# A transformer block in hand-written engine orders: the first and last rounds written out anew

## What is computed

```python
ada = silu(c) @ W_ada + b_ada
shift_msa, scale_msa, gate_msa, shift_mlp, scale_mlp, gate_mlp = jnp.split(ada, 6, axis=-1)
h = _modulate(_layernorm(x), shift_msa, scale_msa)
x = x + gate_msa * _attention(h, W_qkv, b_qkv, W_proj, b_proj)
h = _modulate(_layernorm(x), shift_mlp, scale_mlp)
mlp = jax.nn.gelu(h @ W_fc1 + b_fc1, approximate=True) @ W_fc2 + b_fc2
x = x + gate_mlp * mlp
```

## Time and profile before

| | us |
|---|---|
| median of 3 runs | 1245.8 (1245.76 to 1247.27) |
| the profiled execution's own time | 1245.94 |
| its span | 1244.2 |
| TensorE busy | 1189.1 (96%) |
| VectorE busy | 902.8 (73%) |
| ScalarE busy | 866.3 (70%) |
| GpSimd busy | 541.5 (44%) |

### The profile page before, as it was taken

One profiled execution on the slowest core, in us unless ns is written; L12 is line 12 of the kernel. 1 busy time (PEld: TensorE's weight loads), 2 busy tenths in 40 slices (PEclk: granted clock), 3 DMA queues, 4 the chain that ended last, 5 costly groups with the idle time before them and its releaser, 6 DMA issues.

```text
span 1244.2 us, 27564 instructions
## 1 busy us (share of the span) xinstructions
PE 1189.1 (96%) x9863; PEld 1074.2 (86%) x9863; DVE 902.8 (73%) x1928; ACT 866.3 (70%) x1485; POOL 541.5 (44%) x557
## 2 busy tenths in 40 slices
PE   5877899999999999999999999999999999999987
PEld 5655799999999999999999999999999999998777
DVE  5367777777787777777877777778777877776642
ACT  3186777777777777777777777777777777777721
POOL 3001344455444444544444455444444444444454
PEclk9689999999999999999999999999999999999999
DMA  9344454555554555554454555545455555454220
GB/s 261 111 129 142 145 169 153 165 163 162 164 167 136 161 159 166 165 164 159 154 157 157 160 165 161 167 157 162 147 157 164 162 165 164 149 160 143 96 67 20
DMA packets 134330, 188.91 MB, mean 152 GB/s; under 512 B 24544, under 2 KB 102422, under 8 KB 133947
## 3 DMA queue, kind: packets, MB, share of 16 engines
q1 hardware_dynamic: 134195, 187.15, 47.6%
HBM read 121.92 MB, written 64.63 MB: 150 GB/s over the span
## 4 chain that ended last, share of the span: by engine, by line
PE 88%; DMA 3%; SPq 3%; ACT 2%; DVE 1%; issue 1%; POOL 1%; POOLq 0%; ACTq 0%; DVEq 0%
PE x_bank L585 11%; PE a_bank L677 10%; PE score_bank L615 10%; PE st_bank L632 9%; PE turn_bank L644 9%; PE b_bank L677 8%; PE b_bank L691 6%; PE b_bank L692 6%; PE b_bank L693 6%; PE a_bank L658 5%; PE x_bank L598 4%; SPq L432 1%; PE x_bank L563 1%; PE a_bank L563 1%; DMA o_rows<-on 1%
## 5 line engine op out<-in xcount | busy, mean ns | idle before, releaser
L943 DVE TENSOR_REDUCE mx<-score_bank 128x2 f32<-128x512 f32 x512 | 342.5, 686 | 110.0 <-PE score_bank L615 107.5
L762 ACT ACTIVATE e<-st_bank 128x1024 f32<-128x1024 f32 x256 | 262.6, 1026 | 136.0 <-PE st_bank L632 134.3
L1095 POOL TENSOR_TENSOR gl<-gl_raw,gh 128x512 fp32r<-128x512 f32 (+1 forms) x160 | 193.9, 1220 | 223.2 <-DVE gh L1013 223.2
L755 ACT CAST ql<-mxt 4x256 fp32r<-4x256 f32 x512 | 206.2, 403 | 11.6 <-DVE mxt L957 4.9
L615 PEld LDWEIGHTS score_bank<-kl,ql 122*128 122x128 f32 x1024 | 148.1, 192 | 43.7 <-issue 23.9
L615 PE MATMUL score_bank<-kl,ql 122*128 122x256 f32 x1024 | 175.4, 294 | 8.5 <-DMA ql<-zeros 6.2
L691 PE MATMUL b_bank<-w,gh 128*128 128x288 f32 x576 | 175.0, 304 | 2.9 <-POOL gl L1095 1.5
L632 PE MATMUL st_bank<-ql,kl 122*128 122x512 f32 x512 | 166.8, 407 | 11.0 <-ACT e L762 6.3
L692 PE MATMUL b_bank<-w,gh 128*128 128x288 f32 x576 | 171.1, 297 | 0.0
L693 PE MATMUL b_bank<-w,gl 128*128 128x288 f32 x576 | 170.9, 297 | 0.0
L644 PE MATMUL turn_bank<-e,ve 128*32 128x256 f32 x2048 | 123.8, 382 | 2.1 <-ACT e L762 2.1
(11 more groups left out here) (144 smaller groups left out, 2490.3 us busy)
## 6 DMA issues: line engine op xcount, KB each, us to landing
qk_rows<-qst SPq DMA_DIRECT2D x128, 256.0 KB, 5.4
ql<-qk_rows SPq DMA_DIRECT2D x384, 72.0 KB
kl<-qk_rows SPq DMA_DIRECT2D x384, 72.0 KB
o_rows<-on SPq DMA_DIRECT2D x128, 128.0 KB
gate<-gates SPq DMA_DIRECT2D x32, 432.0 KB, 4.7
xin<-in_x SPq DMA_DIRECT2D x32, 288.0 KB, 5.7
x<-in_x SPq DMA_DIRECT2D x32, 288.0 KB, 2.9
out<-x SPq DMA_DIRECT2D x32, 288.0 KB, 4.4
```

The lines of the kernel that those rows point to most:

```text
L755: last = nc.scalar.copy(rows[:, :, :, t, a, :], src)
L762: nc.scalar.activation(e[:, j % 4, :, :, :].rearrange("p u i l -> p (u i l)"), st_bank[:, :, :, :].rearrange("p u i l -> p (u i l)"), ACT. ...
L943: nc.vector.tensor_reduce(mx[:, j // HP, i, :, col:col + 1], score_bank[i][:, :].rearrange("p (t l) -> p t l", t=NT), AX.X, ALU.max).then_ ...
L1095: nc.gpsimd.tensor_tensor(gl[:, cols], g[:, cols], gh[:, cols].bitcast(F32), ALU.subtract).then_inc(g_lo, 1)
```

## The change

Each engine gets two more lists, a head with explicit batches for everything that rounds -2 to 2 did, and a tail with batches counted from the end for everything from round 30 on. `run` walks the head, then the old list for k = 3 to 29, then the tail. The steps in head and tail are the same as before but for these:

- The late prologue pieces become steps: `mod` and `gate2`, `gate5` on TensorE, `round` on ScalarE, `split`, `gates` and `mod` on VectorE.
- qk part 1 of batch 0 goes to b_bank. Part n of batch 0 waits for n // 2 drained parts.
- qk of every batch waits for the high part of its operand; only the fifth matmul waits for the low part, and the seventh for the remainder.
- Six of the first half's 12 row reads of batch 0 (its k rows) are started by ScalarE, as steps `qkr`.

```diff
-def run(order, steps):
+def run(head, order, tail, steps):
 
-    first = -max(off for _name, off, _n in order)
-    last = B - min(off for _name, off, _n in order)
-    for k in range(first, last):
+    for name, b, n in head:
+        steps[name](b, n)
+    last = B - (TAIL_PERIODS if tail else min(off for _name, off, _n in order))
+    for k in range(HEAD_PERIODS, last):
         for name, off, n in order:
             if 0 <= k + off < B:
                 steps[name](k + off, n)
+    for name, b, n in tail:
+        steps[name](B + b, n)
...
+        FIRST_LO = 4
+
+        def qk_bank(b, n):
+
+            return b_bank if b == 0 and n == 1 else x_bank
...
+        def qk_row(b, n):
+
+            half, m = n // READS, n % READS
+            slot, _use = half_use(b, half)
+            w, i, r = m // 6, m // 3 % 2, m % 3
+            part = ((0, 0, 1), (0, 1, 0))[w][r]
+            c0 = half * HALF_ROWS + (w * 2 + i) * D * HP
+            row = (0, HB)[i] + D * r
+            to = ql[row:row + D, slot, i, :, :] if w == 0 else kl[row:row + D, slot, :, :]
+            return (to.rearrange("p j l -> p (j l)").bitcast(F32),
+                    qk_dram[b % 2, part, c0:c0 + D * HP, :].rearrange("(d j) l -> d (j l)", j=HP))
...
+                if b == 0 and 6 <= n < 12:
+                    return
+                to, src = qk_row(b, n)
+                sp.dma_start(to, src).then_inc(qk_rows[slot], 16)
...
+            def second_mod(_b, _n):
+                pe.wait_ge(ada_rest, 16 * 3)
+                mod_columns(1)
+
             def gate_rows(v, k):
-
+                if k == 0:
+                    pe.wait_ge(ada_rest, 16 * 3)
+                    if v == 5:
+                        pe.wait_ge(x_drained, USE_QK + 2)
...
-                pe.wait_ge(x1_lo, b + 1)
-                pe.wait_ge(x1_rem, b + 1)
-                pe.wait_ge(x_drained, X_USES * b + USE_QK + n)
-                tiles, _rows, _ps = qk_tiles(n)
+                pe.wait_ge(x1_hi, 2 * b + 1)
+                pe.wait_ge(x_drained, X_USES * b + USE_QK + (n if b else n // 2))
+                tiles, _rows, _ps = qk_tiles(b, n)
+                bank = qk_bank(b, n)
                 for k, c in enumerate(tiles):
                     pr = products(xh1, xl1, xr1, wq)
                     for i, (xa, wa) in enumerate(pr):
-                        last = nc.tensor.matmul(x_bank[:, k * L:(k + 1) * L], wa[:, c * P:(c + 1) * P], xa,
+                        if n == 0 and k == 0 and i == FIRST_LO:
+                            pe.wait_ge(x1_lo, b + 1)
+                        if n == 0 and k == 0 and i == len(pr) - 1:
+                            pe.wait_ge(x1_rem, b + 1)
+                        last = nc.tensor.matmul(bank[:, k * L:(k + 1) * L], wa[:, c * P:(c + 1) * P], xa,
                                                 start=(i == 0), stop=(i == len(pr) - 1))
...
+            def first_k_rows(b, n):
+                if n == 0:
+                    for c in range(3):
+                        act.wait_ge(qk_stored[c], 16)
+                    act.wait_ge(consts, ROWS_SET)
+                to, src = qk_row(b, n + 6)
+                nc.scalar.dma_start(to, src).then_inc(qk_rows[0], 16)
```

Of the lists, two rows each of TensorE's head and tail:

```diff
+PE_HEAD = [
+    ("xt", 0, 0), ("xt", 0, 1), ("qk", 0, 0), ("qk", 0, 1), ("qk", 0, 2), ("gate2", 0, 0), ("v", 0, 0), ("v", 0, 1),
+    ("xt", 1, 0), ("xt", 1, 1), ("gate2", 0, 1), ("qk", 1, 0), ("s", 0, 0), ("gate2", 0, 2), ("gate5", 0, 0),
...
+PE_TAIL = [
...
+    ("st", -1, 4), ("fc2", -4, 5), ("lt", -3, 1), ("st", -1, 5), ("st", -1, 6), ("fc1", -3, 0), ("st", -1, 7),
+    ("fc1", -3, 1), ("pv", -1, 1), ("fc1", -3, 2), ("fc1", -3, 3), ("fc1", -3, 4), ("fc2", -3, 0), ("proj", -2, 0),
```

More of the change, by code:

```diff
@@ L220, in dit_block @@
         ada_mod = sem("ada_mod")
-        ada_gate = sem("ada_gate")
+        ada_gate = {v: sem(f"ada_gate{v}") for v in (2, 5)}
         gates_ready = sem("gates_ready")
@@ L552, in gate_rows @@
                 if k == 2:
-                    last.then_inc(ada_gate, 1)
+                    last.then_inc(ada_gate[v], 1)
             pe.wait_ge(ada_first, 16 * 4)
@@ L618, in s @@
                     last.then_inc(s_full[i], 1)
-                if b == 0 and j == 0:
-                    for k in range(3):
-                        gate_rows(5, k)
             def st(b, j):
@@ L733, in qk @@
             def qk(b, n):
-                tiles, rows, ps = qk_tiles(n)
+                tiles, rows, ps = qk_tiles(b, n)
                 for c in tiles:
@@ L764, in st @@
                                      ACT.Exp, scale=SCALE).then_inc(e_ready, 1)
-                if b == 0:
-                    for i in range(N_FIRST + j, N_FIRST + j + 1 if j < PAIRS - 1 else len(loads)):
-                        round_weights(i)
             def pv(b, half):
@@ L804, in fc1 @@
                                      ).then_inc(drained, 1)
-            run(ACT_ORDER, {"xt": xt, "qk": qk, "v": v, "mb": mb, "st": st, "pv": pv, "oh": oh_copy, "lt": lt, "fc1": fc1})
+            def first_k_rows(b, n):
[5 more added lines that the diff above has]
+                nc.scalar.dma_start(to, src).then_inc(qk_rows[0], 16)
+            run(ACT_HEAD, ACT_ORDER, ACT_TAIL, {"round": lambda _b, i: round_weights(N_FIRST + i), "qkr": first_k_rows,
+                            "xt": xt, "qk": qk, "v": v, "mb": mb, "st": st, "pv": pv, "oh": oh_copy, "lt": lt, "fc1": fc1})
         @block.vector
@@ L934, in qk @@
                                         ).then_inc(x_drained, 1)
-                if b == 0 and n == QK_PARTS - 1:
-                    modulation(1)
             def head_max(b, h):
@@ L945, in head_max @@
                                         AX.X, ALU.max).then_inc(s_max[i], 1)
-                if b == 1 and i == 1:
-                    for k in range(N_FIRST + j, N_FIRST + j + 1 if j < PAIRS - 1 else len(loads)):
-                        split_weights(k)
-                if b == 0 and h == 3:
-                    gates()
             def mt(b, half):
@@ L1020, in sum2 @@
                                         ).then_inc(b_drained, 1)
-            run(DVE_ORDER, {"ln1_stats": ln1_stats, "ln1_apply": ln1_apply, "xt": xt, "qk": qk, "max": head_max, "mt": mt, "rcp": rcp,
+            run(DVE_HEAD, DVE_ORDER, DVE_TAIL, {"mod": lambda _b, _n: modulation(1), "gates": lambda _b, _n: gates(),
+                            "split": lambda _b, i: split_weights(N_FIRST + i),
+                            "ln1_stats": ln1_stats, "ln1_apply": ln1_apply, "xt": xt, "qk": qk, "max": head_max, "mt": mt, "rcp": rcp,
                             "om": scale, "ol": ol_rem,
@@ L1108, in sum2 @@
                                         ).then_inc(fc2_added, 1)
-            run(POOL_ORDER, {"ln1_stats": ln1, "ln2_stats": ln2, "xt": xt, "lt": lt, "ol": ol_sub, "proj": proj,
+            run(POOL_HEAD, POOL_ORDER, POOL_TAIL, {"ln1_stats": ln1, "ln2_stats": ln2, "xt": xt, "lt": lt, "ol": ol_sub, "proj": proj,
                              "bias": bias,
```

107 lines of the change are left out of this document (87 added, 20 removed), and 74 rows, old and new, of tables (ACT_HEAD, ACT_TAIL, DVE_HEAD, DVE_TAIL).

## The result

The changed kernel takes 1233.6 us (median of 6 runs, 1228.32 to 1236.28) where the kernel before takes 1245.8 (6 runs, 1240.65 to 1247.27): a ratio of 0.990, 95% interval 0.9875 to 0.993. The gain is 12 us; 26 were forecast, and 1233.6 is above the range of 1208 to 1232. The profiled execution is the fastest of the six, 1228.32 with a span of 1226.5.

What follows compares the result with a forecast made beforehand. TensorE's work was taken to bound the kernel (busy 1189.1 of 1244.2 us), with the losses to win back in head and tail. 1245.9 − 19 (head) − 7 (tail) = 1220 us; 8 in 10 range 1208 to 1232.

Steps and rivals of the forecast that it cites:

- The head: Rounds before the body: denser order brings earlier scores, first st and later halves; forecast gain 19 us.
- The walk: Step-by-step timing of head and tail, each step waiting for bank, operand and engine; head gains 22 us, tail 8.1.
- The 3 us taken off for what the walk leaves out: Head: allowance for waits, late transfers and SyncE's queue, between nothing and 8 us, cutting 22 us to 19.
- covers those copies and 3.7 us more: Head: the modulation's 4.9 us, moved ahead of first st, cover ScalarE's row copies and 3.7 us more; st at 57.7.
- The body: Rounds 3 to 29: order unchanged, TensorE busy throughout, 961 to 963 us long.
- The tail: After the body: batch 31's scores and pv ahead of older fc2; walk gains 8.1 us, forecast 7.
- At 54.5: Tail: the last pv ends 54.5 us after the body's end instead of 65.9; 50.3 by work alone.
- Losses that remain: Tail: 3.6 us ahead of batch 30's fc1, 0.6 per bank turn, 2 around the last turns; last matmul at 109.
- SyncE's queue or the first reads bind: Rival, 12%: SyncE's queue or the first reads limit the head; head gains 10, tail 4, time 1232 us.
- The gaps close fully: Rival, 18%: with the clock up sooner, head gains 26 and tail 9; time 1211 us.
- That the written order changes nothing: Rival, 3%: half-to-half chain is a true minimum; only 5 us of head and 1 of tail stay; 1245 us.
- that TensorE waits in every round: Rival, slower, 4%: body entered with an engine a step behind, TensorE waiting in all 27 rounds; at 1.3 us each, 1255.

Runs made afterwards that it cites:

- e11: The changed kernel as it is, timed again and traced a second time: 1233.65 us, 0.9905 of the kernel before.
- e3: Changed kernel with all 12 row reads of the first half started by SyncE, none by ScalarE: 1235.39 us, 0.991 of the kernel before.
- e5: Changed kernel with SyncE's tail reordered, batch 30's om, ol and proj moved earlier, its turns spread between fc2 pieces of 29: 1234.48 us, 0.9908.
- e6: New head, old tail with proj of 31 ahead of fc2 of 30 and its reads and splits earlier (a mended tail): 1228.82 us, 0.9874.
- e13: New head and old tail, with proj of batch 30 moved behind the last pv of 31 on TensorE: 1232.74 us, 0.9889.
- e7: New head with the second modulation back between batch 0's second and third qk part, plain old tail: 1222.32 us, 0.9824.
- e12: Repeat of the new head with the modulation back between the qk parts and the plain old tail: 1224.06 us, 0.9833.
- e9: Changed kernel, new tail included, with only the second modulation back between the second and third qk part: 1231.47 us, 0.9891.
- e2: Kernel before with only the new order from round 30 on, its head untouched: 1249.43 us, 1.004 of the kernel before.
- e4: Changed kernel with only SyncE's stores and reads for batches 30 and 31 reordered in the new tail: 1234.3 us, 0.9913.
- e1: Changed kernel with all five tail lists emptied, so new head and plain old tail: 1225.52 us, 0.9844.
- e8: New head with the modulation back between qk parts, old tail with proj of 31 ahead of fc2 of 30 (a mended tail): 1229.61 us, 0.9868.
- e10: Repeat of the new head with the plain old tail, in another set: 1227.9 us, 0.9854.

## Why the prediction was right, and where it failed

**The head was right.** The walk had scores at 40.9, first st at 57.7, the sixth and seventh half at 105.5 and 120.9 and the body at 139; the first trace has 39.93, 56.70, 104.40, 122.21 and 138.7. The forecast was 19 us. The one pair of traces says 22.3, but proj of batch 1 starts at 157.80 and 153.64 in the two traces with the old head and at 138.2 in the mean of nine with the new: 17.5 us. The 3 us taken off for what the walk leaves out were about right.

Two terms inside it were luck. The first scores came 1 us from the forecast by two errors that cancel: the last k read went out at 34.27, not near 37.7, but landed after 5.6 us, not 3.2. And a good part of the gain came through the clock. The windows from 15.6 us to proj of batch 1, before and after:

```profile
15.60:157.80 142.20, 110.47 (x745) 89.42 (x746) 86.61 (x182) 76.32 (x135) 25.91 (x28) 0.88 0.48 149
15.60:135.49 119.89, 101.75 (x743) 79.90 (x743) 84.43 (x178) 76.56 (x135) 24.36 (x27) 0.94 0.58 171
```

The idle time fell by 13.6 us and the busy time, for the same work, by 8.7, at a mean granted clock of 0.94 instead of 0.88. The walk had priced everything from 46 us on at the full clock. The first trace bears it out (half clock until 46.2), the others do not: e11 has half clock up to 60.9 and e3, e5, e6 and e13 have a stretch between 82 and 95.

One judgement was wrong: the modulation "covers those copies and 3.7 us more". Those 3.7 us then lay on the path, and its old place between the qk parts costs the scores nothing that the traces show (e7, e12, e9). And the earlier trace rows do not tie the clock to the busy share as closely as the prediction's reading has it: a mean of 0.89 stands also at 27.06 busy of 31.20, and 24.04 of 35.40 has 0.95.

**The body** was to be unchanged. Between proj of batch 1 and of 28 it is 1.3 to 2 us longer in the two traces (963.2 and 963.9 against 961.9); of this 1.3 is one round (below).

**The tail is the step that failed**: forecast −7, and the new order costs 4.2 us alone (e2) and 6 to 7 beside the old one under the new head. The prediction put the tail's work at 96 us, in 117.2 us up to the last matmul: 21 us of losses. Its walk ended at 109, so it kept 13 of them. The first trace of the changed kernel has 119.7 (1222.4 less 1102.7), 23.7 of losses, 10.7 above the walk. Two terms share them about equally.

- *"At 54.5" for the last pv.* It came at 59.5 (1162.2 less 1102.7), 5.0 late. The walk allowed 4.2 us over the bare work of 50.3. In the trace TensorE is idle for 5.4 us of this stretch, where the kernel before is idle for 2.6, and busy for 54.1, 3.8 more than priced. The kernel before shows the same surplus, 63.3 busy for 60.0 priced, so the walk could have seen it. In the second trace it came later still, and proj of 30 with it (70.0 behind proj of 28, against 68.3).
- *"Losses that remain", behind the last pv.* The "8.6 us after the pv" are for the end of proj of batch 30, which the read of o waits for. By the prediction's own prices its first matmul stands 5.4 behind the pv, so at 59.9, and 49 us remain to "the last matmul at 109": some 41 of work and 8 of losses. It did start 5.5 behind the pv, but from there it took 54.8. The gaps named, 3.6 ahead of fc1 of 30 (3.43 measured), 0.6 at bank turns (0.62), 2 around the last turns (1.27), hold one by one. They were not all: TensorE waits 1.28 between the two turns of 30 and 0.56 and 0.74 ahead of the two pieces of proj of 31, 9.6 in all, and 3.4 us of half clock cost 1.7 more.

What the runs show in place of the 8 us gained: the idle time behind proj of 30 is not the order's. It is 9.3 us before, 9.6 with the new tail and 8.1 to 10.6 in all fifteen traces. What runs there is a chain, proj, norm, turns, remainders and fc1 of batch 30, which a_bank's order puts ahead of proj of 31, then the same for 31, and there is no third batch's work to lay over it. What the order does change is the idle time ahead of proj of 30: 2.4 us before and 2.4 to 2.9 with the old tail, 5.1 to 7.6 with the new one. It bought a last pv 6.4 us earlier (59.5, before 65.9) with proj of 30 5.2 later (65.0, before 59.8). e4 and e5 exclude the order of SyncE's stores and reads of batch 30 and 31 and the late splits. Not tested are the order of the row reads, for which the scores wait 1.8 us there, and an a_bank that takes proj of 31 ahead of fc1 of 30.

The prediction also put the gap behind the last pv down to the transfers. They set proj of 31 before, together with 5.7 us of GpSimd's subtractions, which follow the landed factors in the chain of the earlier trace rows:

```profile
1203.22 4.24 POOL gl L1095 x3
1207.46 1.42 POOL ol L1082
```

But when it was freed from them fc1 of 30 stood there instead: proj came 30.4 us behind the pv, not 25.8.

**The clock.** The median of the changed kernel is 5.3 us above its first profile. The second trace, of an execution 4.1 us slower, has 10.2 us of half clock behind the body instead of 3.4 and is 1.5 us longer there; the rest is its later body. An order by work alone did not keep the clock up: behind the body the traces of the plain old tail have no half clock, or 3.4 us with the modulation back, those of the new tail 3.4 to 10.2, e13 6.8, and the two mended tails 10.2. From proj of 28 to the last matmul the two traces of the changed kernel have 2.4 us more of idle time than those of the old tail, and 2.5 and 4.1 us more of busy time for the same matmuls, most of it half clock. What the order does without the clock is seen in e2 beside the kernel before, both with 6.8 us of half clock: 3.7 us longer, 3.0 of it idle.

**The sum** in terms measured: −17.5 for the head, +1.3 to +2 for the body, +3.7 for the tail (proj of 28 to the last matmul, 124.1 in e2 against 120.4) is −12.5 to −11.8; measured −12.2. Such an agreement is partly luck, as single traces scatter by several us.

**The rivals.** "SyncE's queue or the first reads bind" gave the time nearly right, 1232, for a wrong reason: the head did not suffer, and neither e3 nor e4, which change what the queue holds up, changes the time. "The gaps close fully" wanted 26 us from the head and 9 from the tail; the head gave 17.5 (22.3 in the one pair) and the tail none. That the written order changes nothing, and that TensorE waits in every round, are excluded by the starts and by the body's 962.54 busy of 964.0.

## What to carry to other kernels

When the last batches are reordered, find the event from which the rest is a chain with nothing to lay over it, here proj of the last batch but one, and add up TensorE's idle time on both sides of it in the old trace. Here the idle time behind it stayed within 8.1 to 10.6 us whatever the order, so only moving the event earlier could gain, and the new order moved it later. A walk that keeps 13 of the old trace's 21 us of losses must be able to say which of the others are gone, one by one. And take two traces of each kernel before a term is read from their difference.

## What the runs showed of the hardware

One VectorE instruction takes 0.8 to 1.1 us longer once in the body, in some builds and not in others, and in all but one of those builds at the same place. In the changed kernel:

```profile
383.06 1.54 DVE L1167 TENSOR_TENSOR orem_raw<-orem_raw,rcb_rem 119x256 f32<-119x256 f32 x1
```

and in the kernel with the old tail, in the same round:

```profile
385.86 0.41 DVE L1090 TENSOR_TENSOR orem_raw<-orem_raw,rcb_rem 119x256 f32<-119x256 f32 x1
```

The exponential behind it is late, an st waits 1.12 us for it, and the seventh round takes 36.92 us instead of 35.63. It is there in both traces of the changed kernel and in e2, e3, e5 and e13 (in e4 a later round is as long), and not in the kernel before, e1, e6, e7, e8, e9, e10 or e12. The same instruction also takes 1.5 us in the emptying stage of the kernel before (at 1148.91). The instructions up to there are the same in e1 and the changed kernel; the cause is open.

The scatter of the head was larger than I had thought: the same steps brought the first scores between 39.93 and 44.11 us.
